# Two narrow attention stages of an eight-stage kernel: VectorE's row maxima first, its normalisation behind the masks, GpSimd's row addition one pair later

## What is computed

```python
h = layernorm(xr, ln_s, ln_b)
q = split_heads(h @ wq + bq)                       # (16, 16, 128, 16)
k, v = split_heads(kv_in @ wk + bk), split_heads(kv_in @ wv + bv)   # kv_in: h, or the context
scores = einsum('bhqd,bhkd->bhqk', q, k) / sqrt(16.0)
scores = scores * mask - 10000.0 * (1.0 - mask)
probs = softmax(scores, axis=-1)
ctx = merge_heads(einsum('bhqk,bhkd->bhqd', probs, v))
xr = xr + ctx @ wo + bo
```

## Time and profile before

| | us |
|---|---|
| median of 3 runs | 2441.27 |
| lowest, highest | 2440.56, 2449.61 |
| the profiled execution, its own time | 2456.72 |
| its span from the first to the last instruction | 2454.6 |

### The profile page before, as it was taken

How to read it: one execution, slowest core, us unless ns; L and a number is a source line. 1 busy time by engine, 2 the same in 40 slices (tenths; PEclk the granted TensorE clock), 3 DMA queues, 4 the chain that set the end, 5 groups by cost and what they waited for, 6 DMA issues and landing times. The chain is left out here.

```text
span 2454.6 us, 40922 instructions
## 1 busy us (share of the span) xinstructions
PE 2146.2 (87%) x15416; PEld 1882.6 (77%) x15416; DVE 1411.2 (57%) x2772; ACT 958.7 (39%) x2642; POOL 559.8 (23%) x358
## 2 busy tenths in 40 slices
PE   5886787598999999999899999999798968888886
PEld 3664565497889999998789999999698846766775
DVE  4876577524545544554545555555323766877786
ACT  3665466554423333333423333333354322323332
POOL 3442434254200000000300000000053223433331
PEclk8998898798999999999999999999899977877887
DMA  4000100120000000002100000001100000000000
GB/s 147 2 0 1 35 14 4 53 86 7 5 1 5 4 4 4 4 30 78 41 5 5 4 4 4 0 4 41 62 1 9 26 5 1 5 5 4 4 5 13
DMA packets 34347, 45.24 MB, mean 18 GB/s; under 512 B 2144, under 2 KB 26304, under 8 KB 33984
## 3 DMA queue, kind: packets, MB, share of 16 engines
q1 hardware_dynamic: 34240, 43.78, 5.3%
HBM read 33.28 MB, written 2.10 MB: 14 GB/s over the span
## 5 line engine op out<-in xcount | busy, mean ns | idle before, releaser
L693 ACT ACTIVATE arena<-banks 128x512 f32<-128x512 f32 x128 | 72.9, 596 | 416.4 <-PE banks L574 413.7
L686 ACT ACTIVATE arena<-banks,arena 128x129 f32<-128x129 f32 x512 | 180.7, 375 | 135.9 <-DVE arena L737 135.9
L362 DVE TENSOR_TENSOR x_new<-x,banks 128x512 f32<-128x512 f32 x32 | 22.0, 687 | 368.0 <-PE banks L606 236.5
L606 PE MATMUL banks<-arena 128*128 128x256 f32 x1024 | 230.9, 384 | 0.0
L501 POOL TENSOR_TENSOR w_hT_lo<-arena,w_hT_hi 128x512 fp32r<-128x512 f32 x16 | 21.2, 1324 | 902.1 <-ACT w_hT_hi L661 902.1
L606 PEld LDWEIGHTS banks<-arena 128*128 128x128 f32 x1024 | 192.9, 191 | 36.1 <-issue 10.9
L756 DVE COPY arena<-banks 128x512 f32<-128x512 f32 x128 | 88.5, 692 | 210.0 <-PE banks L584 210.0
L1118 ACT ACTIVATE arena<-arena 128x128 f32<-128x128 f32 x512 | 162.2, 392 | 63.1 <-DVE arena L1197 63.1
L931 POOL TENSOR_TENSOR arena<-arena 128x1024 f32<-128x1024 f32 x64 | 151.8, 2392 | 123.4 <-DVE arena L1188 123.4
L1009 PE MATMUL banks<-ident,arena 128*128 128x128 f32 x512 | 92.3, 309 | 80.2 <-ACT arena L1126 70.2
L116 PE MATMUL banks<-w_hT_lo,w_hi 128*128 128x256 f32 x512 | 152.0, 297 | 6.8 <-POOL w_hT_lo L501 6.8
(11 more groups left out here) (273 smaller groups left out, 5889.9 us busy)
## 6 DMA issues: line engine op xcount, KB each, us to landing
arena<-ctx_t SPq DMA_DIRECT2D x32, 256.0 KB, 2.5
arena<-in_L_xattn_wq SPq DMA_DIRECT2D x8, 512.0 KB, 4.4
arena<-in_L_xattn_wk SPq DMA_DIRECT2D x8, 512.0 KB, 5.5
arena<-in_L_xattn_wv SPq DMA_DIRECT2D x8, 512.0 KB, 6.7
arena<-in_L_xattn_wo SPq DMA_DIRECT2D x2, 2048.0 KB, 12.6
x<-in_x SPq DMA_DIRECT2D x4, 512.0 KB, 5.5
arena<-in_L_xattn_w SPq DMA_DIRECT2D x2, 1024.0 KB, 11.2
ctx_t<-in_ctx_t SPq DMA_DIRECT2D x1, 2048.0 KB, 12.5
```

Source lines behind the costliest of these rows:

```text
L606: mm = pe.matmul(at, headT[:, h, b * P:(b + 1) * P], wo[:, h, :], start=False, stop=(h == H - 1))
L686: done = act.activation(prob[:, b, i, :], score_tile(c, j), ACT.Exp, scale=SCALE, bias=shift[:, b, i:i + 1], accum_out=total[:, b, i:i + 1])
```

## The change

In `narrow_attention` only:

- GpSimd adds the rows of pair p-1 instead of p between its two `add_less`, and those of the last pair behind the loop.
- `residual` writes the new rows to `core.x` and their moments to `core.mv` at once. Before, it wrote `core.x_new` and `core.mv_new`, and two more instructions copied them.
- VectorE's body has another order in both halves: `row_max`, `divide`, `mask_scores`, and only then `normalise` or `residual` and `copy_k`.
- VectorE's loop is written out for all eight pairs.

```diff
             def body(p, par):
                 if within(p, 1):
                     add_less(p + 1, 1 - par, 0)
-                add_row(p)
+                if not first(p):
+                    add_row(p - 1)
                 if within(p, 1):
                     add_less(p + 1, 1 - par, 1)
...
             for p in range(NP):
                 body(p, p % 2)
+            add_row(NP - 1)
...
             def residual(p):
                 dve.wait_ge(out_ok, p + 1)
                 dve.wait_ge(x_row_ok, p + 1)
-                wait(dve, stat, p * (2 * PAIR + 1))
-                dve.tensor_tensor(core.x_new[:, :, :], x_row[:, :, :], MISC[:, :].rearrange("p (b d) -> p b d", b=PAIR), ALU.add).then_inc(added, 1)
+                rows = slice(p * PAIR, p * PAIR + PAIR)
+                dve.tensor_tensor(core.x[:, rows, :], x_row[:, :, :], MISC[:, :].rearrange("p (b d) -> p b d", b=PAIR), ALU.add).then_inc(added, 1)
                 dve.wait_ge(added, p + 1)
-                row_stats(core, dve, stat, p, p * (2 * PAIR + 1))
+                for b in range(PAIR):
+                    dve.bn_stats(core.stats[:, b, :], core.x[:, p * PAIR + b, :]).then_inc(stat, 1)
+                dve.wait_ge(stat, p * PAIR + PAIR)
+                for b in range(PAIR):
+                    dve.bn_aggr(core.mv[:, p * PAIR + b, :], core.stats[:, b, :])
 
             def body(p, par):
                 for b in range(PAIR):
-                    if b == 0 and within(p, 2):
-                        normalise(p + 2)
+                    if b == 0:
+                        row_max(p, par, 1)
+                    elif within(p, 1):
+                        row_max(p + 1, 1 - par, 0)
                     if b == 1:
                         divide(p, par, 0)
                     elif not first(p):
                         divide(p - 1, 1 - par, 1)
                     if within(p, 1):
                         mask_scores(p + 1, 1 - par, b)
+                    if b == 0 and within(p, 2):
+                        normalise(p + 2)
                     if b == 1 and not first(p):
                         residual(p - 1)
-                    if b == 0:
-                        row_max(p, par, 1)
-                    elif within(p, 1):
-                        row_max(p + 1, 1 - par, 0)
                     if b == 1 and within(p, 2):
                         copy_k(p + 2, par)
...
-            over_steps(dve, body)
+            for p in range(NP):
+                body(p, p % 2)
```

## The result

| | median us | lowest to highest | ratio to before, 95% interval |
|---|---|---|---|
| before | 2445.44 | 2440.56 to 2452.31 | |
| changed | 2502.84 | 2502.18 to 2503.59 | 1.0233 (1.0202 to 1.0263) |

The change makes the kernel 57 us slower, 2.3%. The profiled execution of the changed kernel took 2502.18 us, its span is 2500.5 us. Between the two profiled spans, 2454.6 and 2500.5, lie 46 us; up to the first instruction of the third stage it is 49.2 us (480.6 and 529.8 us from the start), and the six stages that weren't changed took 3.3 us less.

The account below looks back on a forecast made before the run. VectorE's late maxima were taken to bound the kernel, making ScalarE and TensorE wait and lowering TensorE's clock. Per stage 29.4 + 8.2 + 0.1 - 8.3 = +29.4 us, twice +59: 2441.3 + 59 = 2500 us, range 2454 to 2522.

Parts of the forecast that it names:

- low clock: TensorE behind its wait for normalise: 5 us of work at half speed, +2.5 us in six places per stage.
- the collision: VectorE's two normalise instructions alternate with GpSimd's two add_less on shared ports: up to 4.5 us instead of 0.7.
- Second half: From U, division (p,0), to the next division (p,1): shrinks from 15.0 to 11.3 us.
- First half: From T, division (p-1,1), to division (p,0): grows from 10.4 to 20.1 us, as ln_transpose waits for normalise.
- First pair: Start of each stage up to division (0,0): late normalise and a slower path behind it, +8.2 us in all.
- Last pairs: Pairs 6 and 7, which have no normalise: gains, among them -5.4 and -2.0 us; -8.3 with the last residual's copies.
- The five cycles: Division (0,1) to (5,1) in each stage: 31.4 us per cycle against 25.5, +29.4 us per stage.
- Rival A: GpSimd blocks only the first normalise instruction, VectorE keeps its turn: 2.4 us less in twelve places, 2471 us; chance 0.12.
- B: Rival: TensorE's clock isn't lowered, with the port as forecast: -30 us, 2470 us; chance 0.12.
- C: Rival: normalise meets no add_less, so TensorE's wait is short: 2454 us, or 2424 if the clock holds; chance 0.06.
- D: Rival: only the maxima counted, as if ln_transpose were covered: cycle 21.2 us, 2381 us; chance 0.03.
- the later row addition: GpSimd's row addition for p-1 behind the first add_less, before the residual that reads it: nobody waits.

Follow-up runs that it names:

- e1: Changed kernel with normalise(p+2) put back first in VectorE's body, ahead of the maxima (p,1); 2417 us, ratio to before 0.9885.
- e6: Kernel before with only normalise(p+2) moved behind the masks; 2545 us, ratio to before 1.0403.
- e4: Changed kernel with GpSimd's additions cut to one head of eight in each instruction; 2459.97 us, ratio to before 1.0061.
- e12: Changed kernel with 18 additional matmuls on TensorE ahead of each ln_transpose from pair 2 on; 2483.03 us, ratio to before 1.0144.
- e5: Changed kernel with 14 additional matmuls on TensorE ahead of each ln_transpose from pair 2 on; 2479.15 us, ratio to before 1.0125.
- e8: Kernel before with only VectorE's loop written out; 2439 us, ratio to before 0.9967.
- e7: Kernel before with the changed kernel's residual (no copies) and its written-out loop, order of VectorE's steps as before; 2396 us, ratio to before 0.9792.
- e9: Kernel before with only the maxima (p+1,0) moved ahead of division (p,0); 2401 us, ratio to before 0.9807.
- e2: e1 with the maxima (p,1) moved back behind the division and the masks; 2382 us, ratio to before 0.9746.
- e10: Changed kernel with normalise(p+2) between the division and the masks, ahead of add_less; 2425.43 us, ratio to before 0.991.

## Why the prediction was right, and where it wasn't

- Forecast 2500 us, measured 2502.84. The path was the forecast one: division, masks, `normalise` beside `add_less`, `ln_transpose`, low clock, division. e1 and e6 show the place of `normalise` by taking it away and by adding it alone; e4 shows the collision, e12 and e5 the clock.
- Second half: forecast U + 11.3, measured 11.3, with `copy_k` waiting 1.08 us for `project_k`.
- First half: forecast T + 20.1, measured 18.9 in the self- and 19.2 in the cross-attention. The mis-sized term is the collision. I let `normalise` and `add_less` follow one another, 4.5 us in all; but each `normalise` instruction ended only 0.14 us behind the `add_less` that blocked it, and GpSimd lost nothing (4.69 us for two), so it was 3.87, and `ln_transpose` stood at T + 8.3 instead of 9.1. From there to the division it took 11.1 us in this pair, forecast 11.0. The length of the low clock was partly luck: behind this wait of 7.82 us it lasted for about 6 us, behind the next one, of 7.90, for about 3, and that first half took 17.8 us.
- First pair: forecast +8.2 up to division (0,0). In the self-attention it came +3.4 (58.63 and 62.08 us). Of the difference 2.65 us is nothing that the change did: TensorE had its full clock sooner ahead of the pairs (`project_v` took 1.89 us there, 3.58 before), so that all started earlier; e5, with the same order on VectorE, started as late as before. The other 2.1 us are a smaller collision and a low clock that ended sooner (9.5 us from `ln_transpose` to the division, forecast 11.0). In the cross-attention it came +6.9, counted from the last division of the stage before, and 0.6 more up to (0,1).
- Last pairs: forecast -7.6 without the end of the residual; measured -7.6 in the cross-attention, but -3.5 in the self-attention, where waits of 1.8 to 2.9 us brought the low clock again. The end of the cross-attention, forecast -0.7, came +0.9: VectorE waited 3.5 us for the last projection, 2.1 before.
- The five cycles added 23.3 us in the self- and 25.2 in the cross-attention, forecast 29.4 each. So the two stages together lost 49 us, and not 59. That the median came out within 3 us of the forecast is partly luck: 57 us lie between the medians. No trace here is of an execution of before near its median, so where the other 8 us lie isn't shown; e8, whose two stages match before to 0.2 us, took 2450.12 us in its profile against 2456.72, which puts that difference behind them.
- Rival A (VectorE keeps its turn) falls by the two rows of second instructions; B by the 0.50 of the granted clock; C's mechanism is real, as e4 shows, but `add_less` does run. D priced the gain had `ln_transpose` been covered at 21.2 us and 2381 us; e1 made that case, and it was 23.0 us and 2417. Two terms of D failed there. It had left out the 0.7 us that `normalise` itself takes ahead of the maxima, so the second half was 11.8 us and not 11.3. And a division 1 us late left TensorE idle for 2.1 us, behind which its clock fell in four pairs of five, so the first half was 11.2 us and not 9.9.
- Costing the later row addition as waited for by nobody was right; costing the written-out loop at nothing too.

## What to carry to other kernels

Before a step is moved on an engine that has time to spare, look up who waits for it in order, and compare the moment at which it is wanted with the moment at which it now can start: here 1.9 us behind the division against 4.5. A gain that ends a wait of TensorE of a few microseconds is worth its clock as well, and a new wait costs it as well, so parts of a change are worth trying one by one; here two parts were good (e7, e9), the third undid both, and e2, 2.5% faster than before, needs only that `normalise` and the maxima (p,1) be left where they were.

## What the runs showed of the hardware

- Idle times of TensorE of 2.4 to 2.5 us (e10) were followed by work at the low clock, as those of 4.8 us (e4) and 7.8 us were; behind 1.56 us in e7 they weren't. I had counted on short waits being free of that. Between them the length alone didn't decide: behind 2.0 to 2.1 us in e1 the clock fell in four pairs of five, behind 1.8 to 1.9 us in e5 in two of five. In the changed kernel the same place, pair 6, had 1.90 us of idle time in both stages; the 32 weighings behind it took 1.81 us in the self-attention and 1.08 in the cross-attention.
- The low clock didn't always begin at once: in e10 the four transposes right behind the wait took 0.66 us and the 32 weighings after them 1.91.
- `normalise`, 0.40 us alone, waited in full for the GpSimd instruction under way, lasted up to 2.42 us, and was over about 0.14 us behind it. When both engines had a second instruction in line, GpSimd's went first. `row_max`, a reduction, and `copy_k`, which has an input in PSUM, kept their durations beside the same GpSimd work: 1.19 to 1.22 us and 0.53 to 0.55 us for one instruction in the whole changed kernel.
- Why `normalise` collides and those don't wasn't tried; it has its input and its output in SBUF, like the copies L349 (0.43 to 1.33 us) and L353 (0.17 to 2.04 us) of the kernel before.
